# Mixing whitened images in a one-core Trainium2 kernel: one engine copies both banks of a step, more bank pairs in turn, and GpSimd adds the offset later

## What is computed

```python
# x: (16, 64, 56, 56)
x = x + zca(group_norm(x))               # 16 groups of 4 channels, one 4x4 inverse square root
x = x + window_attention(group_norm(x))  # batch norm, then 7x7-position attention, 16 heads

def zca(x):       # xf: channels x (N*H*W)
    xg = (xf - mean).reshape(16, 4, M)
    cov = einsum('gim,gjm->gij', xg, xg) / M + EPS * eye(4)
    e, v = eigh(cov);  proj = v @ diag(rsqrt(e)) @ v.T
    return einsum('gij,gjm->gim', proj, xg) * weight + bias

def window_attention(x):                 # 16 * 8 * 8 windows of 49 tokens
    q, k = tok @ qk_w.T;  v = relu(tok @ v_w.T)
    return softmax(q @ k.T * DH ** -0.5) @ v
```

## Time and profile before

| | us |
|---|---|
| three timed runs: median (lowest to highest) | 467.7 (466.11 to 467.86) |
| the profiled execution: its own time | 465.49 |
| its span, first to last instruction | 463.8 |
| TensorE busy | 428.6 (92%) |
| VectorE busy | 362.2 (78%) |
| ScalarE busy | 271.1 (58%) |
| GpSimd busy | 192.0 (41%) |
| mean granted TensorE clock | 0.977 of full speed |

### The profile page before, as it was taken

The page is one execution under the profiler, slowest core; times in us unless marked ns, Lnnn a source line. Parts: engine busy times, 40 slices in busy tenths (PEclk is TensorE's granted clock), DMA queues, the critical chain, the costliest instruction groups (busy, mean ns, idle before and its releaser), DMA issues. The chain is left out here.

```text
span 463.8 us, 38693 instructions
## 1 busy us (share of the span) xinstructions
PE 428.6 (92%) x17466; PEld 348.4 (75%) x17466; DVE 362.2 (78%) x1151; ACT 271.1 (58%) x455; POOL 192.0 (41%) x158
## 2 busy tenths in 40 slices
PE   7999925797879999999999999999999999999994
PEld 7898825333657888888888888888888888888883
DVE  1586478777457888888888888888888888888884
ACT  3232300577745676666767676766767676767751
POOL 4072000020133555455545555455545554455422
PEclk9999975999999999999999999999999999999998
DMA  8990000010111424334241424334241524334233
GB/s 297 421 397 12 3 1 0 1 53 19 74 54 57 147 89 147 96 113 147 96 139 69 148 86 148 98 114 148 92 139 70 150 84 149 99 116 147 90 105 72
DMA packets 31564, 52.03 MB, mean 112 GB/s; under 512 B 6176, under 2 KB 21024, under 8 KB 30624
## 3 DMA queue, kind: packets, MB, share of 16 engines
q1 hardware_dynamic: 31520, 51.50, 32.9%
HBM read 12.95 MB, written 12.85 MB: 56 GB/s over the span
## 5 line engine op out<-in xcount | busy, mean ns | idle before, releaser
L340 POOL TENSOR_TENSOR X<-X,otok 128x392 f32<-128x392 f32 x63 | 107.7, 1709 | 159.7 <-DVE otok L735 159.7
L695 DVE TENSOR_REDUCE rmax<-ps 113x16 bf16<-113x784 f32 x128 | 124.1, 970 | 44.6 <-PE ps L870 44.6
L908 PE MATMUL ps<-diag,qk_all 64*49 64x98 f32 x4096 | 128.6, 244 | 0.7 <-ACT prob_all L386 0.7
L908 PEld LDWEIGHTS ps<-diag,qk_all 64*49 64x49 f32 x4096 | 105.4, 120 | 23.8 <-issue 23.6
L922 PE MATMUL ps<-mdiag,sel 64*49 64x98 bf16 x2048 | 111.4, 204 | 0.0
L386 ACT ACTIVATE prob_all<-ps 113x784 f32<-113x784 f32 x128 | 105.5, 825 | 6.1 <-PE ps L922 4.4
L334 POOL TENSOR_SCALAR xs<-X,affined 128x392 f32<-128x392 f32 x64 | 70.0, 1094 | 84.5 <-DVE affined L681 56.1
L401 ACT ACTIVATE vst<-ps 49x256 f32<-49x256 f32 x193 | 73.0, 378 | 54.5 <-PE ps L854 52.1
L393 ACT ACTIVATE qk_all<-ps 128x784 f32<-128x784 f32 x64 | 52.7, 824 | 50.4 <-PE ps L834 50.3
L922 PEld LDWEIGHTS ps<-mdiag,sel 64*49 64x49 bf16 x2048 | 62.9, 99 | 0.9
L953 PE MATMUL ps<-prob_all,vst 113*32 113x49 f32 x4096 | 58.8, 208 | 2.8 <-issue 2.8
(11 more groups left out here) (155 smaller groups left out, 393.6 us busy)
## 6 DMA issues: line engine op xcount, KB each, us to landing
diag<-qk_all SPq DMA_DIRECT2D x256, 98.0 KB
out<-X SPq DMA_DIRECT2D x30, 392.0 KB, 4.2
X<-x_in SPq DMA_DIRECT2D x7, 1024.0 KB, 16.3
X<-x_in SPq DMA_DIRECT2D x7, 544.0 KB, 16.9
X<-x_in SPq DMA_DIRECT2D x4, 256.0 KB, 3.6
out<-X SPq DMA_DIRECT2D x2, 294.0 KB, 3.8
X<-x_in SPq DMA_DIRECT2D x2, 192.0 KB, 4.5
out<-X SPq DMA_DIRECT2D x2, 98.0 KB, 3.3
```

What stands on the lines that cost most here:

```text
L340: g.tensor_tensor(rows_of(u), rows_of(u), otok[u % 2][:].rearrange("p k a s -> p k s a"), ALU.add).then_inc(S["x_ready"], 1)
L695: v.tensor_reduce(rmax[u % 3][0:ROW, :, 8 * k:8 * k + 8], ps[0:ROW, B_S:B_S + 2, 0:8 * POS].rearrange("p h (v q) -> p h v q", q=POS), AX.X ...
L908: ins = mm(ps[64 * e:64 * e + POS, B_ST + hh, col:col + 2 * POS], qk[u % 3][r, g, k, 2 + x_, :], diag[u % 3][r, e::2, g, k, x_, :], start= ...
```

## The change

- A step's two banks are copied by one instruction of one engine, without the offset: ScalarE for two steps of three up to step 13 and then for every even step, VectorE for the others (`by_act`). Each copy is 128 x 784 elements.
- `B_MIX` names three bank pairs in turn for steps 0 to 19 (4, 6, 2, from step 14 on with 0 in place of 2), then 4 and 6, and 2, 4, 6, 2, 4, 2, 4, 2 for the last eight. A step waits for the last step that used its own pair.
- The offset's small matmul moves from step 1 to the place of the sums, now step 4; no copy waits for it. The second group norm subtracts the offset from its mean instead (new line after `dvecd`), since what lies in `X` is without it.
- GpSimd adds the offset to the weighted values `otok` before it adds these to `X`: one more instruction and a wait for it in each `add`. For the last unit, which VectorE adds, GpSimd adds it to `X` once (`settle`).
- The places of the projections and scores move (14, 17; 20, 23; 26), and `keep_v(0)` is cut in two, around step 20's copy.

```diff
-AT_SUMS, AT_AFFINE = 3, 10
-AT_QK, AT_S, AT_MT = (15, 18), (24, 27), 30
+AT_SUMS, AT_AFFINE = 4, 10
+AT_QK, AT_S, AT_MT = (14, 17), (20, 23), 26
...
-        B_MIX = [4 if n % 2 == 0 else 6 if n < MIX - 4 else 2 for n in range(MIX)]
+        B_MIX = [(4, 6, 2)[n % 3] for n in range(12)] + [4, 6, 0, 4, 6, 0, 4, 6] + [4, 6, 4, 6] + [2, 4, 6, 2, 4, 2, 4, 2]
...
+        by_act = [n for n in range(MIX) if (n % 3 < 2 if n < 14 else n % 2 == 0)]
...
+        def mixed_rows(n):
+
+            p, ii = divmod(n, QI)
+            return (X[:, p, :].rearrange("p (a m i w) -> p i m a w", a=WS, m=2, i=QI)[:, ii],
+                    ps[:, B_MIX[n]:B_MIX[n] + 2, 0:392].rearrange("p m (a w) -> p m a w", a=WS))
...
+            def settle(u):
+
+                p, m, ii = place(u)
+                g.tensor_scalar(rows_of(u), rows_of(u), dvecd[:, m, p:p + 1], None, ALU.add).then_inc(S["settled"], 1)
...
             def add(u):
+                p, m, ii = place(u)
                 pool.wait_ge(S["o_ready"], u + 1 + CREDIT["o_ready"])
+                g.tensor_scalar(otok[u % 2][:], otok[u % 2][:], dvecd[:, m, p:p + 1], None, ALU.add).then_inc(S["moved"], 1)
+                pool.wait_ge(S["moved"], u + 1)
                 g.tensor_tensor(rows_of(u), rows_of(u), otok[u % 2][:].rearrange("p k a s -> p k s a"), ALU.add).then_inc(S["x_ready"], 1)
...
             def mix(n):
-                p, ii = divmod(n, QI)
+
                 act.wait_ge(S["mix_ps"], n + 1)
-                for m in range(2 if n in act_both else 1):
-                    ins = a.activation(X[:, p, :].rearrange("p (a i w) -> p i a w", a=WS, i=NW)[:, QI * m + ii],
-                                       ps[:, B_MIX[n] + m, 0:392].rearrange("p (a w) -> p a w", a=WS), ACT.Identity,
-                                       bias=dvecd[:, m, p:p + 1])
-                ins.then_inc(S["mix_act"], 1)
+                out, in_ = mixed_rows(n)
+                a.activation(out, in_, ACT.Copy).then_inc(S["mix_act"], 1)
...
-                if n == 4:
+                if n == 7:
                     act.wait_ge(S["var2_ready"], 1)
                     a.activation(std[:], var[:], ACT.Sqrt).then_inc(S["std2_ready"], 1)
...
             def mix(n):
-                p, ii = divmod(n, QI)
+
                 dve.wait_ge(S["mix_ps"], n + 1)
-                v.tensor_scalar(X[:, p, :].rearrange("p (a i w) -> p i a w", a=WS, i=NW)[:, QI + ii],
-                                ps[:, B_MIX[n] + 1, 0:392].rearrange("p (a w) -> p a w", a=WS),
-                                dvecd[:, 1, p:p + 1], None, ALU.add).then_inc(S["mix_dve"], 1)
+                out, in_ = mixed_rows(n)
+                v.tensor_copy(out, in_).then_inc(S["mix_dve"], 1)
...
+            chain(v.tensor_tensor(mean2[:], mean2[:], dvec[:], ALU.subtract))
...
             u = UNITS - 1
             dve.wait_ge(S["o_ready"], UNITS + CREDIT["o_ready"])
+            dve.wait_ge(S["settled"], 1)
...
                 pe.wait_ge(S["amat_ready"], p + 1)
-                if n >= 2:
-                    mixed(pe, n - 2, 0)
-                    mixed(pe, n - 2, 1)
-                if n == MIX - 3:
+                if n == 2:
+                    pe.wait_ge(S["d_ready"], 1)
+                if n == 14:
+                    pe.wait_ge(S["dd_ready"], 1)
+                    pe.wait_ge(S["affine_ready"], 3)
+                for m in [m for m in range(n) if B_MIX[m] == B_MIX[n]][-1:]:
+                    mixed(pe, m)
+                if n == 24:
                     pe.wait_ge(S["v_ready"], 1)
```

More of the change, by code:

```diff
@@ L196, in conv_preact_kernel @@
             "sums_ready gmean_ps var_ready std_ready vec_ready vec4_ps cov_part cov_ps row_ready full_ps "
-            "pw_ready dv_ps d_ready dd_ps dd_ready affine_ready affine_ps "
+            "pw_ready dv_ps d_ready dd_ps dd_ready settled moved affine_ready affine_ps "
             "amat_ready bnvar_ready mix_ps mix_act mix_dve ag_ps sums2_ready gmean2_ps var2_ready std2_ready "
@@ L220, in give, with mixed @@
                 eng.sem_inc(S[n], CREDIT[n])
[L222 to L228, removed]
-            else:
-                after(eng, "mix_dve", by_dve.index(n) + 1)
+        by_act = [n for n in range(MIX) if (n % 3 < 2 if n < 14 else n % 2 == 0)]
+        def mixed(eng, n):
+            if n in by_act:
+                after(eng, "mix_act", by_act.index(n) + 1)
+            else:
+                after(eng, "mix_dve", n + 1 - sum(m <= n for m in by_act))
+        def mixed_rows(n):
+            p, ii = divmod(n, QI)
+            return (X[:, p, :].rearrange("p (a m i w) -> p i m a w", a=WS, m=2, i=QI)[:, ii],
+                    ps[:, B_MIX[n]:B_MIX[n] + 2, 0:392].rearrange("p m (a w) -> p m a w", a=WS))
         def place(u):
@@ L345, in _ @@
                     normalise(i + 3)
-                elif i + 3 == UNITS:
+                if i + 3 == UNITS - 1:
+                    settle(i + 3)
+                if i + 3 == UNITS:
                     pool.wait_ge(S["st_ps"], KH * (UNITS - 4) + 1)
@@ L394, in keep_qk, with keep_v @@
                              ).then_inc(S["qk_head" if u < 2 else "qk_ready"], 1)
-            def keep_v(u):
+            def keep_v(u, part=None):
                 act.wait_ge(S["v_ps"], u + 1)
                 after(act, "pv_ps", u - 2)
-                for half, e in ((1, 0), (0, 0), (0, 1), (1, 1))[0:4 if u == 0 else 3]:
+                for half, e in ((1, 0), (0, 0), (0, 1), (1, 1))[(0 if part is None else 2 * part):(3 if part is None else 2 * part + 2)]:
                     ins = a.activation(*values_of(u, half, e), ACT.Relu)
@@ L416, in _ @@
                 if n == AT_S[0]:
[L417 to L421, removed]
+                    keep_v(0, 0)
+                if n == AT_S[0] + 1:
+                    keep_v(0, 1)
+                if n in by_act:
+                    mix(n)
+                if n == 26:
+                    mixed(act, 26)
                     a.activation(ps[:, B_ST:B_ST + 2, :], diag[0][:].rearrange("p j g k a s -> p (j g k a s)")[:, 0:1024].rearrange(
@@ L651, in _ @@
             chain(v.tensor_tensor(t84[:], ag[:, :, 1:], a4[:], ALU.mult))
-            chain(v.tensor_reduce(t8[:], t84[:], AX.X, ALU.add))
-            mix(0)
+            v.tensor_reduce(t8[:], t84[:], AX.X, ALU.add)
             chain(v.scalar_tensor_tensor(sd[:, 0, :], dvec[:], float(HW), ag[:, :, 0], ALU.mult, ALU.add))
@@ L739, in _ @@
             dve.wait_ge(S["zeros_ready"], 3)
-            for n in range(13, MIX):
+            for n in range(17, MIX):
                 if n in AT_S:
@@ L744, in _ @@
                     spread_max(0)
-                mix(n)
+                if n not in by_act:
+                    mix(n)
             for i in range(0, UNITS + 1):
@@ L1002, in _ @@
             pe.wait_ge(S["psum_zero"], 1)
-            pe.wait_ge(S["mix_act"], MIX)
-            pe.wait_ge(S["mix_dve"], len(by_dve))
+            mixed(pe, MIX - 2)
+            mixed(pe, MIX - 1)
             def rest(i):
```

33 lines of the change are left out of this document (15 added, 18 removed).

## The result

The changed kernel takes **470.65 us** (median of 5 runs, 469.99 to 471.67), the kernel before 466.89 in the same job (5 runs, 466.11 to 467.86): a ratio of 1.0082 [1.0057, 1.0106], 3.8 us **slower**. The forecast of 464.3 and its range (462.5 to 467.2) missed it; the rival on the other side, late tokens, came true. The profiled execution took 469.99 us (span 468.3, before 463.8).

A forecast was written before the change was run, and what follows sets the result against it. TensorE bounds the steady attention; in mixing engines wait in turn for bank pairs. Mixing -3.9 and the end +0.5 give -3.4 us, from 467.7 to 464.3 us; range 462.5 to 467.2.

The forecast's parts named there:

- late tokens: Rival: in the attention TensorE waits for GpSimd's tokens in every second unit; 471.8 us at the upper bounds; chance 0.12.
- GpSimd's new instruction: In each attention unit, one more 392-element instruction: 1.0 us, range 0.34 to 1.09, at no cost to TensorE.
- The cover: In the attention, instruction and wait may take about 1.07 us at no cost before TensorE wants the tokens; they take 1.06.
- The rival's own formula: Late tokens: if instruction and wait exceed 1.07 us by d, d/2 is lost per unit over some 60 units.
- The stores: In the attention, issued up to 0.7 us later, pushing the last diag DMA to 306.0, before its use at 306.31: no cost.
- Mixing: The stage before the steady attention: whole-step copies of 0.82 and 0.97 us on three bank pairs end it 3.9 us earlier.
- the new wait ahead of step 10: In mixing, TensorE waits 1.3 us for scale and shift, in place of the wait for the offset.
- The give-back in the first pass: Rival: TensorE's waits in its first attention pass lengthen and cancel mixing's gain; 468.2 us; chance 0.09.
- The end: After GpSimd's last add, the final store is issued 0.45 us later, counted as 0.5 us lost.

The follow-up runs named there:

- e3: The changed kernel with GpSimd's queue reordered, the offset instruction, then normalise, then the add to X: 487.42 us, ratio 1.0448.
- e7: The reordered kernel of e3 with each store issued behind the next unit's diag DMAs instead of ahead of them: 464.87 us, ratio 0.9966.
- e6: The changed kernel with its one-operation offset instruction on 294 of the 392 elements: 466.81 us, ratio 0.9999.
- e1: The kernel before with only the new one-operation GpSimd instruction, adding zeros, and its wait in each add: 475.54 us, ratio 1.0201.
- e10: The kernel before with the extra GpSimd instruction in two-operation form, adding zeros, and its wait: 468.08 us, ratio 1.0052.
- e8: The changed kernel with two-operation offset instructions in add and settle, and ScalarE's square root one copy earlier: 462.01 us, ratio 0.9918.

## Why the prediction was wrong

- **GpSimd's new instruction: the step that failed.** "I take 1.0, near that row, and keep 0.34 to 1.09." It took 1.26, above the upper bound. I had bounded it by `normalise` "with two operations and strided tokens", taking one operation and contiguous data for reasons why it must be cheaper. Contiguous data are cheaper (0.67 with two pointers against 1.09 strided), but one operation is dearer by 0.6. The range had no room for that, since the bound rested on the argument and not on a row with one operation. With a ceiling set well beyond the nearest row, the slower side would have had far more than 0.08.
- **The cover: a slip in the sum.** The tokens were said to be wanted at 305.88 less 0.2, and `normalise` to end at 304.53: that leaves 1.15 us, not the 1.07 that the text went on with. The runs show some 1.17. So the forecast's 1.06 was inside the cover by 0.1, and "cover nearly used up" rests on the slip.
- The Trainium skill (GPSIMD Engine Reference, Performance pitfalls for Q7 kernels) puts contiguous elements at about 1.9 cycles. I turned that into an estimate of 0.77 (with the wait of 0.06 that would have left 0.24 of the 1.07, not 0.3). The two-operation form comes near it (0.67), the one-operation form does not (1.26); here the measurement decides.
- **The mechanism of the loss was right**, and stood as a rival: TensorE waits in L918 in every second unit by the amount over the cover. The profile names no releaser for that wait; that it is the tokens follows from the order of the instructions and from e3 and e7, where it goes once `normalise` stands ahead of the add. The rival's own formula, with 1.35 and its 1.07, gives (1.35 - 1.07) / 2 x 60 = 8.4 us; with the 1.15 of its rows it gives 6.0, and the gaps grew by 6.3.
- **The stores: mis-sized.** "It is covered by 0.3 us alone" put them at nothing, and let them come 1.37 late (1.06 and 0.3) at no cost. In e6 they come 1.11 late and cost 0.15 each, some 2 us for 15 stores. And once they come later by a whole `normalise` more (e3), each costs 1.4.
- **Mixing: right in each step.** Copies 0.821 (19 of them) and 0.972 us (13), as taken; root at 88.23 (88.1), scale and shift at 90.2 (90.2), `affined` 91.38 (91.4), `project_qk(0)` 93.65 (93.6), the `diag` DMAs just in time at 99.46 (99.4), `project_qk(2)` 112.18 (112.0). The gain is 4.0 against 3.9. Only the new wait ahead of step 10 was mis-sized: 1.3 was forecast, and the row has 0.66 by TensorE's modelled ends.
- **The give-back in the first pass: not shown.** The way from `project_qk(2)` to the first GpSimd instruction is 0.65 longer than before, but e1 and e10, with mixing as before, have 0.55 and 0.57, and e8, with the shortest mixing, is 0.2 shorter. So the 0.65 can't be told from scatter.
- **The end.** 0.5 was forecast. VectorE's last `otok` comes 3.30 later than before (461.45 against 458.15), the span ends 4.5 later, so the end itself lost 1.2. The end of the changed kernel:

```profile
460.73 1.62 POOL L353 TENSOR_TENSOR X<-X,otok 128x392 f32<-128x392 f32 x1
462.05 1.02 DVE L772 TENSOR_TENSOR X<-X,otok 128x392 f32<-128x392 f32 x1
462.37 1.20 SPq L275 DMA_DIRECT2D out<-X  x2
463.62 2.33 SPq L275 DMA_DIRECT2D out<-X  x2
```

The forecast had the last pair of stores issued 0.45 later, since the first pair holds the queue for 1.20. It does hold it, and the last pair is issued at 463.62, 1.25 behind the first issue, where it was 1.81 before (459.66 less 457.85). But it then takes 2.33 where it took 1.74, so the four issues end 3.58 behind the first one, and 3.55 before: the gain of the earlier issue is lost. In every profile the span ends 5.9 us after the first of these four issues (457.85 and 463.8 before, 462.37 and 468.3 after), and that issue follows the last GpSimd add, which is 4.57 later. So the end goes by GpSimd's last add; why the second pair takes longer no run shows.

VectorE's add started beside GpSimd's and took 1.02 where it took 0.88 alone. The Trainium skill (SBUF — State Buffer, Who interferes with whom) says that a VectorE instruction with two SBUF inputs contends with a GpSimd instruction that reads SBUF; the trace agrees in the direction, with 0.14 us for 0.30 us side by side (462.05 to 462.35). In e1 it is 0.49 (1.37) for 0.64 us side by side.

**The sum, term by term.** The forecast had -3.9 from mixing and +0.5 at the end. Measured in the profiled executions: +0.3 from a later start of mixing, -4.0 from mixing, +0.65 in the first pass, +6.3 in the gaps between adds and +1.2 at the end, together the 4.5 by which the spans differ; the medians differ by 3.8. The step that failed is the cost of GpSimd's instruction in the attention, taken as nothing; the end and the stores were taken too small as well, and e6 shows that without late tokens, too, the forecast gain isn't there (466.81 against 466.88).

## What to carry to other kernels

Don't bound an instruction by a row of a richer form on the argument that it does less: on this chip's GpSimd the TENSOR_SCALAR with one addition took twice as long as the one with a multiplication and an addition. Where your own sum leaves a new instruction no more than about 0.1 us of cover, a small error in its size is multiplied by the number of units, and the chance of the bad side must say so. And look behind "100% busy": count matmuls in a fixed stretch, or the distance between two recurring instructions.

## What the runs showed of the hardware that I had not expected

- GpSimd TENSOR_SCALAR, 128x392 f32, contiguous: one operation (an addition) 1.261 us (pointer) or 1.190 (immediate); two operations 0.595 (immediate and pointer) or 0.673 (two pointers). With 294 elements, one operation: 1.022. An estimate from the two sizes (1.261 and 1.022): 2.4 ns an element and 0.3 us fixed. Strided, in place: 2.05 against 1.01.
- A store of two DMAs ahead of the four `diag` DMAs in SyncE's queue costs some 1.4 us in most units when the `diag` DMAs are needed at once (units of 6.6 us for 5.21, e3), and nothing when it is issued behind them (e7).
- The last four store issues of the program take 3.55 to 3.58 us from the first on, whether the second pair is issued 1.81 or 1.25 us after the first.
